# Attention and local-attention layers on one NeuronCore: the values product turned round, probabilities normalised on VectorE, TensorE passes and engine queues reordered

## The reference, cut to what matters

```python
def _layer(x, wqkv, qs, ksc, wo, lg, lb, w1, b1, w2, b2):
    q, k, v = jnp.split(shift_token(x) @ wqkv, 3, axis=-1)      # 8 heads of 64
    q = l2norm(q) * qs; k = l2norm(k) * ksc
    q, k = rotary_xpos(q, k)
    # local_attention: windows of 128 rows, keys of the own and the previous window
    sim = jnp.einsum('bhwid,bhwjd->bhwij', bq * 8, bk)
    attn = jax.nn.softmax(jnp.where(mask, -max, sim), axis=-1)
    out = jnp.einsum('bhwij,bhwjd->bhwid', attn, bv)
    x = x + o @ wo
    h = layer_norm(shift_token(x)) * lg + lb
    a, g = jnp.split(h @ w1 + b1, 2, axis=-1)                   # 682 columns each
    return x + (a * jax.nn.gelu(g)) @ w2 + b2
```

## Time and profile before

| | |
|---|---|
| Time, median of 3 runs | 3229.55 us (3192.76 to 3246.99) |
| Profiled execution: span from first to last instruction | 3224.0 us |
| TensorE busy | 3082.3 us, 96% |
| VectorE busy | 2444.6 us, 76% |
| ScalarE busy | 1877.0 us, 58% |
| GpSimd busy | 1190.4 us, 37% |
| Mean granted TensorE clock | 0.969 of full speed |
| First transposes of the layers' tile 1 (L1277) | about 381 us after the start |

### The profile page before, as it was taken

One profiled execution on the slowest core, in us unless ns is written; L12 is line 12 of the kernel. 1 busy time (PEld: TensorE's weight loads), 2 busy tenths in 40 slices (PEclk: granted clock), 3 DMA queues, 4 the chain that ended last, 5 costly groups with the idle time before them and its releaser, 6 DMA issues.

```text
span 3224.0 us, 71318 instructions
## 1 busy us (share of the span) xinstructions
PE 3082.3 (96%) x23040; PEld 2745.2 (85%) x23040; DVE 2444.6 (76%) x7393; ACT 1877.0 (58%) x4750; POOL 1190.4 (37%) x1303
## 2 busy tenths in 40 slices
PE   8999799999999999999999999999999999999997
PEld 6777588988888898989888888988898888889896
DVE  3566687777777777878777788878787878788885
ACT  3455365665565665656655666656566656566663
POOL 3455343333333333323233334334343344343342
PEclk7799899999999999999999999999999999999998
DMA  4344400000000000000002211001010011010000
GB/s 139 111 138 156 157 25 20 23 24 21 23 24 21 22 20 23 24 21 23 22 23 77 80 42 31 28 26 31 24 30 28 27 31 31 24 31 27 27 28 17
DMA packets 139639, 137.09 MB, mean 43 GB/s; under 512 B 15256, under 2 KB 124912, under 8 KB 137968
## 3 DMA queue, kind: packets, MB, share of 16 engines
q1 hardware_dynamic: 139248, 132.18, 13.0%
HBM read 80.22 MB, written 51.92 MB: 41 GB/s over the span
## 4 chain that ended last, share of the span: by engine, by line
PE 66%; DVE 13%; issue 6%; ACT 2%; DVEq 1%; DMA 1%; POOL 1%; SPq 0%; ACTq 0%; POOLq 0%
PE p_values L1320 11%; PE p_wide L95 10%; PE p_wide L97 9%; PE p_wide L96 9%; PE p_turn L1303 5%; PE p_mixed L95 4%; PE p_mixed L96 3%; PE p_mixed L97 3%; PE p_turn L1277 3%; PE p_score L95 2%; DVE prob L1112 2%; DVE rope_sin L1130 2%; DVE rope_cos L1126 2%; PE p_values L1346 1%; PE p_score L96 1%
## 5 line engine op out<-in xcount | busy, mean ns | idle before, releaser
L984 ACT ACTIVATE prob<-prob,least 128x256 f32<-128x256 f32 (+1 forms) x1024 | 495.8, 489 | 373.3 <-DVE least L1112 373.3
L1112 DVE CUSTOM_DVE_ANT_0 prob<-p_score,mask,inv_norm 128x256 f32<-128x256 f32 (+1 forms) x1024 | 417.0, 464 | 145.7 <-issue 145.6
L1320 PEld LDWEIGHTS p_values<-v,pT 128*128 128x128 f32 x3840 | 456.6, 192 | 50.2 <-issue 32.4
L939 POOL TENSOR_TENSOR inv_norm<-norm_clipped,minus_half 128x8 f32<-128x8 f32 x256 | 445.5, 1740 | 108.1 <-DVE norm_clipped L1141 87.3
L1320 PE MATMUL p_values<-v,pT 128*128 128x64 f32 x3840 | 463.2, 273 | 21.8 <-DVE o L1152 19.7
L95 PE MATMUL p_wide<-hT_h,w_h 128*128 128x256 f32 (+1 forms) x1408 | 408.7, 290 | 15.1 <-DVE gated L1225 12.6
L97 PE MATMUL p_wide<-hT_h,w_l 128*128 128x256 f32 (+1 forms) x1408 | 396.3, 281 | 0.0
L96 PE MATMUL p_wide<-hT_l,w_h 128*128 128x256 f32 (+1 forms) x1408 | 395.8, 281 | 0.0
L999 ACT ACTIVATE pT<-p_turn 128x512 f32<-128x512 f32 (+1 forms) x512 | 266.0, 568 | 174.6 <-PE p_turn L1303 174.6
L1225 DVE SCALAR_TENSOR_TENSOR gated<-p_wide,columns,gelu 128x256 f32<-128x256 f32 (+1 forms) x384 | 184.2, 482 | 231.2 <-ACT gelu L1031 231.2
L95 PE MATMUL p_wide<-wqkv_h,xT_h 128*128 128x512 f32 x768 | 351.4, 458 | 5.0 <-DMA wqkv_l<-w_low 3.8
(11 more groups left out here) (139 smaller groups left out, 8077.8 us busy)
## 6 DMA issues: line engine op xcount, KB each, us to landing
x_tile<-x_rows SPq DMA_DIRECT2D x192, 128.0 KB, 2.1
w_high<-a_wraw_h SPq DMA_DIRECT2D x32, 264.0 KB, 2.2
w_low<-a_wraw_l SPq DMA_DIRECT2D x32, 264.0 KB, 2.5
x_rows<-a_x SPq DMA_DIRECT2D x64, 128.0 KB, 1.7
x_tile<-x_rows SPq DMA_DIRECT2D x128, 64.0 KB, 1.9
mid_rows<-x_mid SPq DMA_DIRECT2D x128, 64.0 KB, 1.6
x_mid_shifted<-mid_rows SPq DMA_DIRECT2D x128, 64.0 KB, 1.9
x_rows<-x_new SPq DMA_DIRECT2D x64, 128.0 KB, 1.7
```

Source lines behind the costliest of these rows:

```text
L939: pool.tensor_tensor(r[:, slot, heads], rt[:, heads], half[:, heads], ALU.pow)\
L984: act.activation(prob[:, h, cols], prob[:, h, cols], ACT.Exp, bias=least[:, h:h + 1], scale=-1.0, accum_out=rsum[:, h:h + 1]).then_inc(act ...
L1112: dve.tensor_tensor_reduce(prob[:, h, cols], p_score[h % 2][:, c0 + cols.start:c0 + cols.stop], mask[:, a.slot(2), cols], r[:, a.slot(2), ...
L1320: ins = pe.matmul(p_val[:, hh * D:(hh + 1) * D], pT[:, group, hh, b], v[:, slot, h * D:(h + 1) * D], start=b == blocks[0], stop=b == block ...
```

## The change

- **Probabilities.** `prob` has two buffers. VectorE multiplies each head's probabilities by the reciprocal row sum in place, one TENSOR_SCALAR of 128x256 per head (`normalised`, after four exponentials each). The two multiplications into `o`, the buffer `o` and its four transposes are gone.
- **Values.** The stationary operand is v (128 keys x 64), the moving one pT (128 queries), and two heads write the two halves of the partitions of `p_val`, so the result is already `oT`.
- **One step later.** `turn_probs` and `values` belong to tile n-2 (`c`) now.
- **Scores.** The three passes of a pair of heads alternate between the two halves of TensorE's rows.
- **FFN tail.** gT_h's tail chunk holds the high part in partitions 0 to 41 and again in 64 to 105, w2's tail the high part over the low part, the rest is zeroed once; two passes of 128 rows instead of three of 42. ScalarE copies one more 42x256 tile per pair, w2's loads are four DMAs instead of two.
- **GpSimd** clips the norms itself (L1141 leaves VectorE) and its work is reordered: k's rotary sum, clip, power and scale come first, then layer-norm, then q's clip and power, then the residual.
- **Orders** within a step, per engine, as in the diff.

```diff
+                def inverse_norms(n):                          # GpSimd
+                    heads = slice(n * H, (n + 1) * H)
+                    pool.wait_ge(dve_ss[n], t.done(1, 1))
+                    pool.sem_inc(pool_took, 1)
+                    pool.tensor_scalar(rt[:, heads], ss[:, heads], NORM_FLOOR, None, ALU.max).then_inc(pool_rt[n], 1)
+                    pool.wait_ge(pool_rt[n], t.done(1, 1))
+                    pool.tensor_tensor(r[:, t.slot(2), heads], rt[:, heads], half[:, heads], ALU.pow)\
+                        .then_inc(pool_r[n], 1)
...
+                if c:                                          # ScalarE, whole order of a step
+                    turned_probs(0)
+                if t:
+                    squares(1, pe_k)
                 if a:
                     act.wait_ge(pe_qT, a.done(1, 1))
...
                 if c:
+                    turned_probs(1)
                 if a:
                     probabilities(0, 4)
                 if t:
+                    squares(0, pe_q)
+                if c:
+                    act.wait_ge(pe_pv, c.done(2, 2))
+                    act.activation(oT_h[:], p_val[:].rearrange("p (k t) -> p k t", t=P), ACT.Copy).then_inc(act_oT, 1)
                 if a:
+                    probabilities(4, 8)
...
+                        if n == HF:
+                            act.wait_ge(pool_zero, 1)
+                            act.activation(gT_h[GR:GR + HR, n], gt[0:HR, n % 3], ACT.Copy)
...
+                def normalised(group):                         # VectorE
+                    heads, cols = slice(4 * group, 4 * group + 4), key_columns(a)
+                    dve.wait_ge(act_exp, a.done(H, 4 * group + 4))
+                    dve.reciprocal(rinv[:, heads], rsum[:, heads]).then_inc(dve_rinv, 1)
+                    dve.wait_ge(dve_rinv, a.done(2, group + 1))
+                    for h in range(4 * group, 4 * group + 4):
+                        p = prob[:, a.slot(2), h, cols]
+                        dve.tensor_scalar(p, p, rinv[:, h:h + 1], None, ALU.mult).then_inc(dve_p, 1)
+
+                if t:
+                    rotary(1, dve_kr, pool_k)
                 if a:
...                                                            # qT_l, kT_l
+                if t:
+                    squared_norms(1)
...                                                            # x_new, layer-norm statistics
                 if a:
                     least_of(0)
...                                                            # h_norm, out_tile
+                if t:
+                    rotary(0, dve_qr, dve_q)
+                if c:
...                                                            # oT_l
                 if a:
+                    normalised(0)
                     least_of(1)
+                if t:
+                    squared_norms(0)
...                                                            # q_rot
                 if c:
...                                                            # x_mid
+                if a:
+                    normalised(1)
                 if st_.even and f:
...                                                            # hT, hT_l (odd steps: xT_l), then the gating
                 def scores(group):                             # TensorE
...
+                    for m in (2 * group, 2 * group + 1):
+                        c0 = m % 2 * 2 * P
+                        for q, k, first, last in ((qT_h, kT_h, True, False), (qT_h, kT_l, False, False),
+                                                  (qT_l, kT_h, False, True)):
+                            for half in range(2):
+                                rows = slice(half * D, (half + 1) * D)
+                                ins = pe.matmul(p_score[half][:, c0 + cols.start:c0 + cols.stop], q[rows, m],
+                                                k[rows, m].rearrange("p b t -> p (b t)")[:, cols],
+                                                start=first, stop=last)
...
                 def values(group):
...
+                    for m in range(2):
                         for b in blocks:
+                            slot = c.slot(4) if b == c.slot(2) else (c.off - 1) % 4
+                            for half in range(2):
+                                h = 4 * group + 2 * m + half
+                                ins = pe.matmul(p_val[half * D:(half + 1) * D, (2 * group + m) * P:(2 * group + m + 1) * P],
+                                                v[:, slot, h * D:(h + 1) * D], pT[:, group, 2 * m + half, b],
+                                                start=b == blocks[0], stop=b == blocks[-1])
...
                 if c:                                          # TensorE, whole order of a step
+                    turn_probs(0)
+                if t:
+                    pe.wait_ge(dve_xT, t.done(1, 1))
...
+                    project(1, p_wide[0], pe_k)
+                if a:
+                    turn_qk()
+                if e:
...
+                    for n in range(HF):
+                        three_pass(pe, p_mix[:, 0:E], (gT_h[:, n, c0:c0 + P], gT_l[:, n, c0:c0 + P]),
+                                   (w2[0][:, n], w2[1][:, n]), n == 0, False)
+                    pe.matmul(p_mix[:, 0:E], gT_h[:, HF, c0:c0 + P], w2[0][:, HF], start=False, stop=False)
+                    pe.matmul(p_mix[:, 0:E], gT_l[:, HF, c0:c0 + P], w2[0][:, HF], start=False, stop=True)\
+                        .then_inc(pe_w2, 1)
+                if c:
+                    values(0)
                 if a:
                     scores(0)
+                if c:
+                    turn_probs(1)
+                if t:
+                    need(pe, dve_qr, t.done(1))
+                    project(0, p_wide[1], pe_q)
+                if c:
+                    values(1)
+                if a:
+                    scores(1)
+                if t:
+                    pe.wait_ge(dve_kr, t.done(1, 1))
+                    project(2, p_wide[0], pe_v, [0])
                 if c:
...                                                            # wo, waits for dve_oT
+                if t:
+                    project(2, p_wide[0], pe_v, [1])
                 if f:
...                                                            # transposes of h_norm, wait for dve_mid; then w1 as before
```

More of the change, by code:

```diff
@@ L967, in step, with probabilities, squares, turned_probs @@
                     turned_x(t)
-                a = st_.tile(1)
+                a, c = st_.tile(1), st_.tile(2)
+                def probabilities(first, last):
+                    cols = key_columns(a)
+                    for h in range(first, last):
+                        act.wait_ge(dve_least, a.done(H, h + 1))
+                        act.activation(prob[:, a.slot(2), h, cols], prob[:, a.slot(2), h, cols], ACT.Exp,
+                                       bias=least[:, h:h + 1], scale=-1.0, accum_out=rsum[:, h:h + 1]).then_inc(act_exp, 1)
+                def squares(n, product):
+                    act.wait_ge(product, t.done(1, 1))
+                    need(act, dve_ss[n], t.done(1))
+                    act.activation(sq[:, n * H:(n + 1) * H], p_wide[1 - n][:].rearrange("p (h d) -> p h d", h=H),
+                                   ACT.Square).then_inc(act_sq[n], 1)
+                def turned_probs(group):
+                    own = blocks_of(c)
+                    keys = own[0] if c.first else slice(0, 2)
+                    for n in range(2):
+                        act.wait_ge(pe_pT, c.done(4, 2 * group + n + 1))
+                        src = p_turn[n][:].rearrange("p (h b t) -> p h b t", h=2, b=2)
+                        act.activation(pT[:, group, 2 * n:2 * n + 2, keys, :], src[:, :, keys, :], ACT.Copy)\
+                            .then_inc(act_pT, 1)
+                if c:
+                    turned_probs(0)
+                if t:
+                    squares(1, pe_k)
                 if a:
@@ new lines, in rotary @@
+                def rotary(n, raised, last):
+                    dve.wait_ge(act_sq[n], t.done(1, 1))
+                    need(dve, last, t.done(1))
+                    if n == 1 and t.is_number(LAYER):
+                        dve.wait_ge(tab_in, 16)
+                    bank = p_wide[1 - n]
+                    src = bank[:].rearrange("p (h s d) -> p h s d", h=H, s=2)
+                    table = tab[:, t.window].rearrange("p c (s d) -> p c s d", s=2)
+                    dve.tensor_tensor(rope_a[:, n], bank[:].rearrange("p (h d) -> p h d", h=H),
+                                      tab[:, t.window, 2 * n].unsqueeze(1).to_broadcast([P, H, D]), ALU.mult)
+                    dst = rope_b[:, n].rearrange("p h (s d) -> p h s d", s=2)
+                    for s in range(2):
+                        ins = dve.tensor_tensor(dst[:, :, s], src[:, :, 1 - s],
+                                                table[:, 2 * n + 1, s].unsqueeze(1).to_broadcast([P, H, D // 2]),
```

(17 more changed lines are left out.)

277 lines of the change are left out of this document (88 added, 189 removed).

## The result

The changed kernel takes 3822.4 us (median of 4 runs, 3813.0 to 3839.0), the kernel before 3226.7 us on the same chip: a ratio of 1.190, 95% interval 1.184 to 1.197. The profiled execution has a span of 3814.6 us, 591 us more than that of before. The forecast was 3860 us.

The account below looks back on a forecast made before the run. TensorE bounds the old kernel; after the change, a loop through VectorE's queue does. 7.2 us chain plus 2.6 us clock, 9.8 us on 64 pairs, is 627 us: 3224 + 627 = 3851 us span, 3860 us median; range 3570 to 4090.

Parts of the forecast that it names:

- The chain: VectorE's queue ahead of `xT_l` and `hT_l`, with its waits, sets the loop: 50.0 us a pair against 42.8.
- the clock term: Halved TensorE clock after waits: 1.6 us for w1 and 1.0 us for k, 2.6 us a pair.
- VectorE's prices: TENSOR_SCALARs 0.30 us apart, 1.4 us a `normalised` group; VectorE's work some 1.2 us more per step.
- TensorE's saving: Values 1.2 us, transposes of `o` 0.4, tail 0.3, score passes nothing: 1.9 us less a step.
- The rival in which TensorE stays the bound: VectorE's queue runs ahead, `hT_l` ready within some 15 us; 3.8 us a pair less, 2985 us; chance 0.06.
- The port: GpSimd's power for q holds up `normalised(1)`, 1.0 us a step: 3990 us; chance 0.16, shared with no column-half overlap.
- The turn of the loop was to stay as it is: At the layers' turn of the tile loop, no added time was forecast.
- the shifted `mid_rows`: Stored some microseconds later and read back by the next step's statistics 6 us into that step; costed at nothing.
- The chain's shares: In the profile after, VectorE was to have the largest share in the chain of waits.

Follow-up runs that it names:

- e3: Changed kernel plus useless identity transposes on TensorE before wo, before x or h_norm is turned, and before w1: 3678.4 us, ratio 1.152.
- e5: Changed kernel with only ScalarE's and VectorE's work reordered, TensorE's program untouched and no instruction saved: 3413.4 us, ratio 1.063.
- e2: Changed kernel with squares of q and turned-values copy ahead of ScalarE's first four exponentials, and least_of(1) ahead of normalised(0) on VectorE: 3739.2 us, ratio 1.168.
- e4: Changed kernel with each group of four normalising TENSOR_SCALARs cut to one single-column instruction, probabilities left unnormalised: 3710.2 us, ratio 1.156.
- e8: Kernel before with only the alternated order of the score passes: ratio 0.9995 (0.996 to 1.003).
- e6: e5 with the two `ln_rstd` instructions moved ahead of k's scaling on GpSimd, nothing else: 3362.7 us, ratio 1.050.
- e11: Changed kernel with the values passes of one column half ahead of the other's instead of alternating: 3913.3 us in its one run.

## Why the prediction was right, step by step

**The chain.** The phases of the predicted loop, in us from the start of a k product, against the pair shown (odd from 1295.03, even from 1315.26):

| | rotary of k | `least_of(0)` done | rotary of q | x_mid done | xT_l or hT_l done | next k product |
|---|---|---|---|---|---|---|
| odd, predicted | 2.35 | 8.25 | 11.8 | 18.3 | 20.0 | 20.0 |
| odd, measured | 2.45 | 8.35 | 12.2 | 18.6 | 20.2 | 20.2 |
| even, predicted | 2.15 | 8.05 | 10.45 | 17.0 | 20.6 | 30.0 |
| even, measured | 3.6 | 9.6 | 12.05 | 18.4 | 22.0 | 33.7 |

The odd step holds. The even step is late by 1.4 us from its first phase on, since its k product ran at the halved clock (2.73 instead of 1.47 us between starts), and by 2.2 us more in w1: both are the clock term, priced apart. With the clock up (e3) the pair takes 50.3 us, and 50.1 on average over eight steps without a turn, where 50.0 was the sum. That the order of the queues makes the loop is shown by e5, two thirds of the slowdown by order alone, most of it by VectorE's (e5 against e2); that it is not mainly the added work, by e4.

**The clock.** 2.6 us a pair were taken. The filled gaps bring 123 us by the ratios, 1.9 us a pair over the whole run, 2.2 us by the traces over eight steps without a turn, and 3.6 us in the pair shown. The cause was right and the size somewhat too high on the average.

**VectorE's prices.** The TENSOR_SCALARs start 0.26 us apart, the lower bound, not 0.30: a group takes 1.27 us (1309.11 to 1310.38) against 1.4. That is 0.3 us less in a step, and the rotary of q, 0.4 us late in the odd step, takes it back. VectorE's work grew by 0.5 us a step, where 1.2 us were worked out.

**TensorE's saving.** A group of 1.02 us against 1.1 taken; the tail 0.25 against 0.3; the score passes nothing (e8). Where the waits are shorter, in e6, eight steps hold 158.5 us of TensorE's work against 172.2 us: 1.7 us a step against 1.9. It exists and is buried under the waits. The rival in which TensorE stays the bound needed hT_l within some 15 us; it came at 22.0.

**The port.** The changed kernel shows GpSimd's power beside the second normalising group at 1313.73:

```profile
1313.46 1.67 POOL L923 TENSOR_TENSOR inv_norm<-norm_clipped,minus_half 128x8 f32<-128x8 f32 x1
```

The mean over its groups of this shape from 1000 to 1800 us is 349 ns:

```profile
L1125 DVE TENSOR_SCALAR prob<-prob,rinv 128x256 f32<-128x256 f32 x216 | 61.7, 349 | 1.9
```

That group takes 1.14 us, as the one at 1309.31 does while GpSimd has nothing. So the power doesn't hold up VectorE and the rival fails. The wide scaling of k does: 1.03 us for 0.34 in e6. The Trainium skill ("SBUF — State Buffer", Who interferes with whom) lets the two engines take the shared pair in turn for a whole instruction; the k scaling's 0.69 us agree, the power's 1.67 us, an instruction of eight columns, do not, and here the measurement decides.

**What was missed.** The turn of the loop was to stay as it is. It doesn't. The step with the turn in it takes 25.8 us, 4.3 to 5.6 us over other odd steps (20.2 and 21.5 us), where before it took 19.8 us, 2.3 over its neighbours. The kernel before at the turn (TensorE's timeline), then the changed one (the whole step, and the same place of the timeline):

```profile
1039.18 0.65 PE L1277 MATMUL p_turn<-ident,q_rot 128*128 128x128 f32 x4 [2.23 <-issue]
```

```profile
1135.40:1161.20 25.80, 18.70 (x131) 15.52 (x131) 14.28 (x48) 11.56 (x29) 7.78 (x9) 0.80 0.08 21
```

```profile
1156.85 1.96 PE L1315 MATMUL p_turn<-ident,prob 128*128 128x128 f32 x8 [3.81 <-issue]
```

TensorE starts up 1.6 us later and at the halved clock behind it. The steps behind the turn give a part back or cost more again, so whole rounds of eight steps tell its price. Without a turn, near the end of the second layer, before and after:

```profile
2968.40:3140.60 172.20, 169.03 (x1331) 152.97 (x1330) 143.72 (x429) 107.29 (x278) 69.33 (x80) 1.00 0.10 28
```

```profile
3514.50:3723.70 209.20, 170.06 (x1290) 145.58 (x1289) 145.78 (x468) 109.55 (x282) 74.00 (x96) 0.90 0.08 23
```

With a turn they take 177.5 and 216.5 us there, the mean of four: 5.3 us for the turn before and 7.3 us now. The 11 turns cost some 22 us more.

The change of the layer costs another 10 us more: its eight steps take 225.5 us, 16.3 over those without a turn, where before it was 178.0 and 5.8. Two waits for loads are seen there; the prediction named only the second, and costed it at nothing. The k product waits 10.28 us for the second layer's weights, where before it waited 3.81 us:

```profile
2024.48 0.77 PE L95 MATMUL p_wide<-wqkv_h,xT_h 128*128 128x512 f32 x1 [10.28 <-DMA wqkv_l<-w_low]
```

and the statistics wait 5.31 us, once, for the shifted `mid_rows`.

**How the errors add up.** A pair costs 9.2 us more than before (52.3 against 43.0), not 9.8, which is some 35 us too much in the forecast. The turns and the change of the layer, some 32 us, were left out of it. And the layers' first tile comes 22 us sooner in the profiled execution (358.4 against 381 us). That last is no work of the change: the mean granted clock of the first 350 us was 0.92 there and 0.87 in the trace of before, and in the other traces of this case that tile comes anywhere between 351 and 412 us. So the chain was forecast well, and that the total is off by just 38 us is partly luck, since errors of both signs meet in it.

The chain's shares were misjudged too: VectorE was to have the largest and has 27%, TensorE 39%. A loop that passes from engine to engine shares itself out among them, and the shares don't tell which of them sets it; TensorE's waits in the pair shown, all for VectorE, and the reordering of e5 do.

## What to carry to other kernels

In a software pipeline whose engines hand each other every tile, lay out the chain from one start of a product to the next with every wait in queue order, before counting work: 1.7 us a step off TensorE and 0.5 us on VectorE gave 19% more time, and the same instructions in another order took two thirds of it back. Order each in-order queue by who waits for the result, and put the work that nobody waits for (here normalising and the sum of q) behind it; look for the same on every other engine and in every phase, since a reorder that reads well on one (q and k turned first) can hold up the next, and one that reads well in the first layer can hold up the second. A gap on TensorE can be paid twice, once as time and once as clock.

## What the runs showed of the hardware that was not expected

- **Column halves overlap when they alternate, and hardly in two runs of eight.** Sixteen passes of 64 stationary and 128 moving columns take 1.02 us alternated, 1.51 us in two runs of eight (e11). Row halves in runs of three already overlap: alternating them brought nothing (0.9995).
- **VectorE's TENSOR_SCALAR with one scalar, in place, 128x256:** a start every 0.26 us, as for 128x128 with two scalars. Twice the elements with one scalar less cost nothing; the two were not varied apart.
- **The port between VectorE and GpSimd** is held by a GpSimd instruction of 128x512 (0.34 us became 1.03 in e6, and 0.35 again where the scaling waits) and not by the power of 128x8, which is longer (1.67 us; a group beside it takes 1.14 us, as without it).
- **Filling TensorE's waits with work of no use** lifts the mean granted clock from 0.894 to 0.979 and brings the ratio from 1.190 to 1.152.
